# A mixture-of-experts layer on one core: tokens scattered as raw rows with their statistics, normalised when their slots are read

## The reference

```
x = x + attention(layernorm(x))          # scores are distances of 3-d positions, causal
n = layernorm(x)
score = softmax(n @ gate.T)              # 8 experts
best two experts per token by score + bias, weighted by score
y = sum over the two of  weight * w2[e] (silu(w1[e] n) * w3[e] n)
z = sw2 (silu(sw1 n) * sw3 n)            # shared expert, inner width 512
x = x + y + z
```

## Time and profile before

| what | value |
|---|---|
| median of 3 runs | 673.12 us (672.82 to 673.82) |
| profiled execution | 675.16 us |
| span of its trace, first to last instruction | 673.4 us |
| PE busy | 560.7 us, 83% of the span |
| DVE busy | 448.1 us, 67% |
| ACT busy | 338.5 us, 50% |
| POOL busy | 216.4 us, 32% |

### The profile page before, as it was taken

The page is one execution under the profiler, slowest core; times in us unless marked ns, Lnnn a source line. Parts: engine busy times, 40 slices in busy tenths (PEclk is TensorE's granted clock), DMA queues, the critical chain, the costliest instruction groups (busy, mean ns, idle before and its releaser), DMA issues.

```text
span 673.4 us, 11259 instructions
## 1 busy us (share of the span) xinstructions
PE 560.7 (83%) x3484; PEld 485.8 (72%) x3484; DVE 448.1 (67%) x1143; ACT 338.5 (50%) x710; POOL 216.4 (32%) x404
## 2 busy tenths in 40 slices
PE   3738899965698994952797989899999999998995
PEld 2727489964658994541676777688888888887884
DVE  4984997888399765967775775444444444444985
ACT  0416998333499851641444444355555555553331
POOL 3061300034132001001774776154545545452000
PEclk9778999968797997977797999899999999999998
DMA  8988000000000004700221222233333333325941
GB/s 280 318 249 3 1 1 1 2 1 0 1 0 1 2 1 149 320 1 8 87 96 55 83 92 87 72 103 103 104 111 103 103 104 104 110 80 174 385 162 62
DMA packets 57127, 62.59 MB, mean 93 GB/s; under 512 B 14736, under 2 KB 50448, under 8 KB 57072
## 3 DMA queue, kind: packets, MB, share of 16 engines
q1 hardware_dynamic: 49216, 43.46, 22.7%
q0 software_dynamic: 6480, 17.77, 7.4%
q10 hardware_dynamic: 1376, 0.66, 0.4%
HBM read 30.50 MB, written 31.37 MB: 92 GB/s over the span
## 4 chain that ended last, share of the span: by engine, by line
PE 40%; DVE 11%; issue 4%; ACT 4%; DVEq 1%; another core or an unknown queue 1%; POOL 0%; ACTq 0%; POOLq 0%
PE bank L1208 11%; PE bank L1210 11%; PE bank L1209 11%; PE bank L1329 2%; PE bank L1345 2%; DVE hf L1138 2%; PE bank L1217 1%; ACT h_hi L891 1%; DVE X L1129 1%; DVE XR L974 1%; DVE h_lo L1149 1%; ACT W_hi L911 1%; DVE XN L974 1%; DVE W_lo L1153 1%; DVE XT_lo L1019 1%
## 5 line engine op out<-in xcount | busy, mean ns | idle before, releaser
L843 POOL DMA_INDIRECT token_out<-YS,to_row x71 | 69.6, 980 | 96.6 <-ACT YS L941 93.0
L827 POOL DMA_INDIRECT slots_in<-XR,slot x64 | 69.4, 1085 | 88.1 <-DVE XR L1108 69.8
L575 PE MATMUL a_bank<-VO,E_hi 128*128 128x258 f32 x272 | 78.6, 289 | 6.6 <-DVE E_lo L482 6.6
L579 PE MATMUL a_bank<-VO,E_lo 128*128 128x258 f32 x272 | 78.2, 288 | 0.0
L577 PE MATMUL a_bank<-VO,E_hi 128*128 128x256 f32 x272 | 78.0, 287 | 0.0
L1179 DVE TENSOR_TENSOR hr<-bank,sr 128x256 f32<-128x256 f32 x71 | 30.1, 425 | 62.0 <-issue 48.9
L1208 PE MATMUL bank<-XT_hi,sw_hi 128*128 128x512 f32 x128 | 53.6, 419 | 13.2 <-DVE XT_lo L1019 11.6
L1208 PE MATMUL bank<-W_hi,XST_hi 128*128 x142 | 62.3, 438 | 0.5 <-DVE XST_lo L1183 0.5
L929 ACT ACTIVATE sr<-bank 128x256 f32<-128x256 f32 x71 | 27.2, 383 | 64.2 <-PE bank L1210 63.4
L575 PEld LDWEIGHTS a_bank<-VO,E_hi 128*128 128x128 f32 x272 | 52.9, 194 | 7.3 <-DVE E_lo L482 7.3
L1210 PE MATMUL bank<-W_hi,XST_lo 128*128 x142 | 56.9, 401 | 0.0
(11 more groups left out here) (227 smaller groups left out, 1621.3 us busy)
## 6 DMA issues: line engine op xcount, KB each, us to landing
XS<-slots_in SPq DMA_DIRECT2D x71, 129.0 KB
YG<-token_out SPq DMA_DIRECT2D x16, 512.0 KB, 7.7
slots_in<-blank SPq DMA_DIRECT2D x7, 1161.0 KB, 14.6
W_raw<-in_wT_dram SPq DMA_DIRECT2D x8, 768.0 KB, 12.5
X<-in_x_dram SPq DMA_DIRECT2D x8, 512.0 KB, 7.7
out_dram<-X SPq DMA_DIRECT2D x32, 128.0 KB, 2.3
token_out<-YS,to_row POOLq DMA_INDIRECT x71, 2.4
slots_in<-blank SPq DMA_DIRECT2D x1, 1032.0 KB, 14.6
```

Source lines behind the costliest of these rows:

```text
L575: pe.matmul(O_ps[Q % 2][j][:, 0:D + 2], E_hi[:, n % NE, cols], VO[:, kt, 0:D + 2], start=(kt == 0), stop=False)
L579: mm = pe.matmul(O_ps[Q % 2][j][:, 0:D + 2], E_lo[:, n % NE, cols], VO[:, kt, 0:D + 2], start=False, stop=(kt == qt))
L827: pool.indirect_dma_start(out=xs, out_offset=bass.IndirectOffsetOnAxis(ap=slot[k][:, t:t + 1], axis=0), in_=XR[:, t % 4, k, :], in_offset= ...
L843: pool.indirect_dma_start(out=ys, out_offset=bass.IndirectOffsetOnAxis(ap=to_row[:, i:i + 1], axis=0), in_=YS[:, i % NYS, :], in_offset=No ...
```

## The change

X is widened by six columns: mean, reciprocal deviation, first expert, own row number, weight of the second choice, and first weight minus second. Both transfers of a tile now read X itself, raw, and XR, `scatter_tile` and `second_row` are gone. A slot's row is normalised on DVE when it is read (`slot_rows`, into XSN), and DVE and POOL work out from the row whether this slot is the token's first or second choice, and from that its target row and weight. The router scores are taken from raw X too, and the mean and deviation are put in afterwards with three instructions on the whole score table, for which PE sums the gate weights once. The loops over groups in this stage are written out on DVE and PE.

```
-N_CHOSEN = 18
-RW = D + 2
+N_CHOSEN = 21
+RW = D + 6
+MEAN, RSTD, FIRST, HOME, W1, DW = range(D, RW)
...
-            act.wait_ge(s_mv, NT)
-            act.activation(std[:, :], mv[:, :, 1], ACT.Sqrt, bias=eps_col[:, 0:1]).then_inc(s_std, 1)
...
             logits_hi(0, 0)
             logits_hi(1, 1)
+            act.wait_ge(s_mv, NT)
+            act.activation(std[:, :], mv[:, :, 1], ACT.Sqrt, bias=eps_col[:, 0:1]).then_inc(s_std, 1)
...
-            logits_xn(0, 0)
...
+            dve.wait_ge(s_gs, 1)
+            dve.tensor_copy(gsum[:, :], gs_ps).then_inc(s_gsum, 1)
...
+            dve.tensor_copy(X[:, :, MEAN], mv[:, :, 0]).then_inc(s_cols, 1)
+            dve.tensor_copy(X[:, :, RSTD], rstd[:, :]).then_inc(s_cols, 1)
+            for G in range(2, NG):
+                logits_lo(G, G % 2)
+                logits_out(G - 2, G % 2)
...
+            done(dve.tensor_tensor(tmp[:, :, :], mv[:, :, 0:1].to_broadcast([P, NT, NX]), over_t(gsum), ALU.mult))
+            done(dve.tensor_tensor(logit[:, :, :], logit[:, :, :], tmp[:, :, :], ALU.subtract))
+            done(dve.tensor_tensor(logit[:, :, :], logit[:, :, :], over_e(rstd), ALU.mult))
...
+                    dve.tensor_scalar(X[:, :, FIRST], red2[:, :], -1.0, float(NX), ALU.mult, ALU.add).then_inc(s_cols, 1)
+                    dve.wait_ge(s_cols, 3)
...
+            for k, out in ((1, X[:, :, W1]), (0, X[:, :, DW])):
+                done(dve.tensor_tensor(tmp[:, :, :], pick[k][:, :, :], score[:, :, :], ALU.mult))
+                done(dve.tensor_reduce(out, tmp[:, :, :], AX.X, ALU.add))
+            done(dve.tensor_tensor(X[:, :, DW], X[:, :, DW], X[:, :, W1], ALU.subtract))
+            dve.wait_ge(s_cols, 3)
             dve.sem_inc(s_slot, 1)
...
             for t in range(NT):
                 for k in range(TOPK):
-                    if k == 0:
-                        pool.wait_ge(s_xr, 2 * t + 2)
-                    else:
-                        pool.wait_ge(s_xr1, t + 1)
...
-                                            in_=XR[:, t % 4, k, :], in_offset=None).then_inc(s_sc[t % 4], 16)
+                                            in_=X[:, t, :], in_offset=None).then_inc(s_sc[t // GT], 16)
...
-                pool.tensor_copy(to_row[:, i:i + 1], XS[:, i % 4, D:D + 1]).then_inc(s_mt, 1)
-                pool.tensor_copy(by_weight[:, i:i + 1], XS[:, i % 4, D + 1:RW]).then_inc(s_mt, 1)
+                pool.wait_ge(s_sel, 2 * i + 2)
+                pool.tensor_tensor(home[:, i:i + 1], back[:, i:i + 1], row[:, HOME:HOME + 1], ALU.add).then_inc(s_meta, 1)
+                pool.tensor_tensor(by_weight[:, i:i + 1], is_first[:, i:i + 1], row[:, DW:DW + 1], ALU.mult)\
+                    .then_inc(s_meta, 1)
+                pool.wait_ge(s_meta, 2 * i + 2)
+                pool.tensor_copy(to_row[:, i:i + 1], home[:, i:i + 1]).then_inc(s_mt, 1)
+                pool.tensor_tensor(by_weight[:, i:i + 1], by_weight[:, i:i + 1], row[:, W1:W1 + 1], ALU.add)\
+                    .then_inc(s_mt, 1)
...
             for i in range(4, NSLOT):
-                sp.wait_ge(s_xsT, i - 3)
+                sp.wait_ge(s_sn, i - 3)
                 sp.wait_ge(s_mt, 2 * (i - 3))
...
+                dve.wait_ge(s_sc[G], 16 * TOPK * GT)
+                xz = X[:, G * GT + 2 * z:G * GT + 2 * z + 2, 0:D]
...
+            def slot_rows(i):
+                dve.wait_ge(s_xs[i % 4], 16 * (i // 4) + 16)
+                if i >= 2:
+                    dve.wait_ge(s_xsT, i - 1)
+                row = XS[:, i % 4, :]
+                dve.tensor_scalar(XSN[:, i % 2, :], row[:, 0:D], row[:, MEAN:MEAN + 1], row[:, RSTD:RSTD + 1],
+                                  ALU.subtract, ALU.mult).then_inc(s_sn, 1)
+                dve.tensor_scalar(is_first[:, i:i + 1], row[:, FIRST:FIRST + 1], which[:, i:i + 1], None,
+                                  ALU.is_equal).then_inc(s_sel, 1)
+                dve.tensor_scalar(back[:, i:i + 1], row[:, FIRST:FIRST + 1], which[:, i:i + 1], -float(P * NT),
+                                  ALU.is_equal, ALU.mult).then_inc(s_sel, 1)
...
+            slot_rows(0)
             for i in range(-3, NSLOT):
+                if i + 4 < NSLOT:
+                    slot_rows(i + 4)
                 if i + 3 < NSLOT:
                     tokens_lo(i + 3, (i + 3) % 2)
```

More of the change, by code:

```diff
@@ L241, in _ @@
             pool.wait_ge(s_const, 8)
+            pool.memset(blank[:, FIRST:FIRST + 1], -1.0).then_inc(s_const, 1)
             pool.affine_select(out=ident[:, :], in_=ident[:, :], compare_op=ALU.not_equal, fill=1.0, base=0,
@@ L613, in attention_and_experts @@
         red2 = sb("red2", [P, NT])
-        meta = sb("meta", [P, NT, TOPK, 2])
+        biased = sb("biased", [P, NT, NX])
+        slot_e = sb("slot_e", [P, NT, NX])
+        total = sb("total", [P, NX, NT])
+        upto = sb("upto", [P, NX, NT])
+        keep = sb("keep", [P, NX, NT])
+        passed = sb("passed", [P, NSLOT, NX])
+        is_first = sb("is_first", [P, NSLOT])
+        back = sb("back", [P, NSLOT])
+        home = sb("home", [P, NSLOT])
         to_row = sb("to_row", [P, NSLOT], u32)
@@ L716, in attention_and_experts @@
         s_slot = sem("f_slot")
-        s_xr = sem("f_xr")
-        s_sc = [sem(f"f_sc{i}") for i in range(4)]
+        s_sc = [sem(f"f_sc{g}") for g in range(NG)]
+        s_gs = sem("f_gs")
+        s_gsum = sem("f_gsum")
+        s_cols = sem("f_cols")
+        s_sel = sem("f_sel")
+        s_sn = sem("f_sn")
         s_wr = sem("f_wr")
@@ L775, in _ @@
             sp.wait_ge(s_T, N_T + KC * HALF)
-            for k in range(4):
-                sp.wait_ge(s_sc[k], 16 * TOPK * NT // 4)
+            for g in range(NG):
+                sp.wait_ge(s_sc[g], 16 * TOPK * GT)
             for k in range(4):
@@ L975, in normalised @@
                                          ALU.subtract, ALU.mult)
-            def logits_xn(G, v):
-                for j in range(GT):
-                    normalised(XN[:, v, j, :], G * GT + j).then_inc(s_xn, 1)
             def logits_lo(G, v):
@@ L1097, in slot_experts @@
                 dve.sem_inc(s_slot, 1)
-            def choice_weights():
-                for k in range(TOPK):
-                    done(dve.tensor_tensor(tmp[:, :, :], pick[k][:, :, :], score[:, :, :], ALU.mult))
-                    done(dve.tensor_reduce(meta[:, :, k, 1], tmp[:, :, :], AX.X, ALU.add))
-            def scatter_tile(t):
-                if t >= 4:
-                    dve.wait_ge(s_sc[t % 4], 16 * TOPK * (t // 4))
-                normalised(XR[:, t % 4, 0, 0:D], t).then_inc(s_xr, 1)
-                dve.tensor_copy(XR[:, t % 4, :, D:RW], meta[:, t, :, :]).then_inc(s_xr, 1)
             def add_routed(g):
@@ L1120, in add_routed @@
                     dve.wait_ge(s_yy, g * 2 + h // 2 + 1)
-                    dve.tensor_tensor(X[:, tiles, :], X[:, tiles, :], YG[:, tiles, 0, :], ALU.add).then_inc(s_y, 2)
+                    dve.tensor_tensor(X[:, tiles, 0:D], X[:, tiles, 0:D], YG[:, tiles, 0, :], ALU.add)\
+                       .then_inc(s_y, 2)
             def add_shared(G, z):
@@ L1222, in logits @@
                 pe.wait_ge(s_xtl, G * KC + 3 * KC)
-                if not (isinstance(G, int) and G == 0):
+                if G > 0:
                     pe.wait_ge(s_lc, G)
@@ L1240, in _ @@
             logits_transpose(1, 1)
+            for c in range(KC):
+                mm = pe.matmul(gs_ps, ones_f[:, :], gate_raw[:, c, :], start=(c == 0), stop=(c == KC - 1))
+            mm.then_inc(s_gs, 1)
             logits(0, 0)
-            with pe.Fori(0, NG // 2 - 1) as k:
-                for v in range(2):
-                    logits_transpose(k * 2 + v + 2, v)
-                    logits(k * 2 + v + 1, 1 - v)
-                    turn_logits(v)
+            pe.wait_ge(s_gsum, 1)
+            for G in range(NG - 2):
+                logits_transpose(G + 2, G % 2)
+                logits(G + 1, 1 - G % 2)
+                turn_logits(G % 2)
             logits(NG - 1, 1)
```

109 lines of the change are left out of this document (37 added, 72 removed).

## The result

The changed kernel takes 718.69 us (median of 4 runs, 716.87 to 722.2) against 673.47 (672.82 to 676.09) for the one before: a ratio of 1.067, 95% interval 1.062 to 1.072. Forecast were 654.6 us and a range of 649.5 to 662.0. The 64 us between the forecast and the result lie in one place. The profiled execution took 722.2 us with a span of 720.5.

A forecast was written before the change was run, and what follows sets the result against it. PE bounds the slots and last stage, a cross-engine chain the scatter stage. Slots starting 19.0 us earlier, plus 0.5, give -18.5: 675.16 becomes 656.7, less 2.04 for the median, 654.6 us; range 649.5 to 662.

The forecast's parts named there:

- First scores 265.85: Second block's start: transposes no longer wait for the statistics, so first scores come at 265.85 instead of 270.94, 5.1 earlier.
- first scatter 313.2: End of the choice: POOL starts its first scatter at 313.2 instead of 317.71.
- `outputs(0)` 316.1: Shared stage's start: after `hf(0)` and `h_lo`, PE goes on at 316.1, 8 us earlier than 324.21.
- The three instructions in the choice: Chain of the choice: three added instructions on 256 elements, each starting 0.46 after the one before, cost 1.4 us.
- the pace of the score stage: Score stage: PE's chain stays as long as before, so pace unchanged; 0 to 2 us gain or loss for written-out loops.
- Scatters at 1.39 us, the last over at 402.1: Scatter on POOL: 64 transfers, nothing to wait for, mean 1.39 us, take 89 us and end at 402.1 instead of 419.66.
- "`slot_rows(0)` ... start at 406.5": Start of the slots: after the last scatter, XS load and `slot_rows(0)`, first transposes at 406.5 instead of 425.51, 19.0 earlier.
- "Does the shared stage end in time?": Shared stage beside the scatters: 4.5 us a chunk, ending at 403.6, 3 us before POOL's line, so it no longer decides.
- The rival of the late shared stage: Shared stage stalls as in ACT's 3.02 us wait, slots start at 409 to 411, about 658 us; chance 0.19.
- The rival of the lock-out: Scatter locked out by every two-input DVE instruction, 29 us on 81, slots at 427.4, 675.5 us; chance 0.03.
- Slots unchanged: Slot stage: 2.58 us of PE a slot, added DVE and POOL work hidden, 0 a slot and 0.5 us once.
- the chance of 0.04 for slower by `meta_of`: Slots: POOL's `meta_of` binds above 0.85 us, eats all 18.5 at 1.12, and gives 678 us at 1.2; chance 0.04.

The follow-up runs named there:

- e9_every4: Changed kernel, but every fourth scatter waits for the landing of the one two before; 666.98 us, ratio to before 0.9826 to 0.9905.
- e2_landed: Changed kernel, but each scatter first waits until the one two before has landed; 665.3 us, ratio to before 0.992.
- e1_paced: Changed kernel, but GpSimd issues scatters a few per chunk, at the pace of the kernel before; 667.06 us, ratio to before 0.9932.
- phase 6: In the first kernel with none of the layer's work: unbroken indirect transfers of 64-byte rows beside straight-line instructions on DVE, ACT and PE; 1.04 us a transfer.
- phase 5 of the second small kernel: No layer work: indirect transfers, every third waiting for the landing of the one two before, beside ScalarE and TensorE; pitch 1.42 us.
- small kernels: Two kernels with none of the layer's work, seven phases each: engines run their own instructions beside GpSimd's transfers, varied in kind or pauses; no total time given.

## Why the prediction was wrong

- **First scores 265.85, first scatter 313.2, `outputs(0)` 316.1.** Measured 265.09, 314.19, 317.48. Right within 1.4 us. The three instructions in the choice took 1.4 as forecast, but the pace of the score stage, which I let stand, did not: the first of them started at 294.73, 4.25 us earlier than the choice did before (298.98), after first scores 5.85 us earlier.
- **Scatters at 1.39 us, the last over at 402.1.** In the changed kernel 1.30, over at 397.19, because DVE stood still and met few of them. With DVE at full speed and no pause at all it would be 1.048 + 0.30 = 1.35, an end near 400 (an estimate from `e9_every4`'s mean).
- **"`slot_rows(0)` ... start at 406.5", 4.4 after the last scatter.** `e2_landed`: from 409.84 to 414.21, 4.4.
- **"Does the shared stage end in time?" 4.5 us a chunk, the end at 403.6.** This is the step that failed: the last shared sum ended at 471.0, 67 us later. It took the pace of a stage in which GpSimd does nothing and set it beside 64 scatters without a pause, as if only DVE's and GpSimd's meetings could couple them; the slowing of all three engines by the run itself was put at nothing. ("Meet only at semaphores", as said of the engines at the top, is not so.) Where the transfers don't stop the engines the step holds: the slots start at 402.01 and 404.04 in the two kernels with plain transfers, and these take 652.44 and 653.75 us, the forecast 654.6. In `e2_landed`, which does the layer's whole work, PE is through with the shared stage at 402.4.
- **The rival of the late shared stage (0.19, about 658)** had the right place and the wrong size, by 60 us. I read ACT's wait of 3.02 us as a stray event, "for it speaks that nothing in the change touches it". It was probably touched: the trace of before has ten scatters in close succession ahead of it,

```profile
341.90 0.96 POOL L827 DMA_INDIRECT slots_in<-XR,slot  x1 [1.40 <-DVE XR L1108]
...
354.01 0.96 POOL L827 DMA_INDIRECT slots_in<-XR,slot  x1 [0.30 <-issue]
361.67 0.96 POOL L827 DMA_INDIRECT slots_in<-XR,slot  x1 [6.69 <-DVE XR L1108]
```

  and none was issued for 6.69 us after them, until the next XR had been made. That this wait is the same slowing is an inference: `e1_paced` shows one like it, 6.37 us after 24 scatters, but the beat of 1.40 us can't be made out in the trace of before. The chunk's coupling that I counted as a cost (69.8 us of POOL's idle time) was also a brake: slower engines, fewer scatters. The change took the brake off, and then the loop turns the other way: slower engines, a DVE that holds off fewer scatters, so a denser run. That this link makes the run denser is an inference from the means of 997 ns against 1,048; the slowing itself is shown with and without DVE.
- **The rival of the lock-out (0.03).** The Trainium skill ("SBUF — State Buffer", "SBUF: two separate sides") has either engine hold the shared ports for its whole instruction. A transfer of 100.85 us beside back-to-back two-operand instructions agrees that one can shut the other out, but it was shut out for some 300 instructions of 0.33 us and not for one, and the 1.04 us of phase 6 shows next to no lock. In this kernel it costs 0.09 us a scatter (1.048 against 0.96), far from the 29 us of this rival.
- **Slots unchanged, and the chance of 0.04 for slower by `meta_of`.** The slots ran at full PE, 181.39 of 182, so this rival fell. (Its price at 1.2 us, 678, is about 1 us low by its own terms.) Slower came by a mechanism that was in none of the cases.

What stays open is what the engines lack. It is not bandwidth, another engine's signal, something that only straight code needs, GpSimd being busy, or, as far as its queues show, a load of instructions from memory; each engine is slowed by itself, and some 20 scatters go by first. The trace has no row that names it. Nor was it tried whether the demand of the engines matters: at 0.46 us idle between scatters (phase 5 of the second small kernel, pitch 1.42) ACT, which had nothing else to wait for, fell to 13 of 34, and at 0.48 (`e2_landed`, pitch 1.52) the layer's kernel lost nothing that shows. That plain transfers don't do it was seen for 64 in 34 us, a time in which 27 scatters would have gone out; a longer run was not tried.

## What to carry to other kernels

When a change takes the waits out from between transfers on GpSimd, ask what those waits held back, and look at all engines, not only at the one that the waits fed: indirect transfers in a run of more than some 15 to 20, with less than about half a microsecond between them, slowed every other engine here; runs of 8 with a pause between still cost a few us. Let each wait for the landing of the one two before it (here 1.067 of the time before became 0.992), and fill the time that this takes with work from elsewhere (0.9835). A wait in the trace without a known releaser, next to a dense run on GpSimd, may be a sample of it; price it by what happens if the run grows, not by how often it occurred.

## What the runs showed of the hardware

- In the small kernels, during 64 indirect transfers with 0.30 us between them, VectorE and ScalarE each run one instruction per 1.40 to 1.43 us from 20 to 30 us on, and TensorE 3 or 4 matmuls with their loads in 10 us, whatever the row's size (64 or 1,048 bytes), in straight code and in loops (there with some 3 us more per turn); ScalarE and VectorE alone as well as together. No packet of the queues of the kind "instruction" moved from 262 to 517 us, in which the loop phase lies. At a pitch of 1.36 us ScalarE runs 11 in 10 us after 50 us, at 1.42 it runs 13, at 1.54 all 34.
- 64 plain transfers of the same bytes from GpSimd (0.547 us each, 234 GB/s) or from SyncE, and memsets on GpSimd, slow none of them.
- TensorE's granted clock was 0.55 in the stalled window (1.2 GHz is 0.50), in which it ran 36 matmuls in 67 us. It was 0.50 from 404 to 412, 0.95 from 412 to 416 and 1.00 from 416 on.
- Two-operand instructions of VectorE without a gap held one indirect transfer of 1,048-byte rows for 100.85 us, and held none of 64-byte rows (1.04 us each). Instructions with one SBUF operand held none (mean 0.98 us against 0.96).
